# Reordering the hand-written instruction streams of a pipelined AdaLN block on one core: four engines' call orders and the banks of shared PSUM units

## The reference

```python
mod = (silu(c) @ wmod).reshape(8, 6, 1, -1)            # sa, ca, ga, sb, cb, gb
h = layernorm(x) * (1 + ca) + sa
q, k, v = rope(h @ Wq), rope(h @ Wk), h @ Wv
ck, cv = compress(k + pe), compress(v + pe)            # 16 tokens into one
imp = (q · ck).mean(heads, queries); idx = top_k(imp, 2)
out = g0 * attend(q, ck, cv) + g1 * attend(q, k[idx], v[idx]) + g2 * window_attend(q, k, v, 128)
x = x + ga * (out @ Wo + bo)                           # g = softmax(h @ Wg + bg)
h = layernorm(x) * (1 + cb) + sb
x = x + gb * (h @ W.T + b + shared(h) + top2_routed(h))
```

## Time and profile before

| what | us |
|---|---|
| median of the three runs (2274.74 to 2276.2) | 2275.06 |
| span of the profiled execution | 2265.8 |
| the profiled execution's own time beside its span: the runs' median less the span | 9.3 |
| TensorE busy in the span | 2108.9 (93%) |
| VectorE busy | 1698.7 (75%) |
| ScalarE busy | 1331.8 (59%) |
| GpSimd busy | 792.1 (35%) |

### The profile page before, as it was taken

The page is one execution under the profiler, slowest core; times in us unless marked ns, Lnnn a source line. Parts: engine busy times, 40 slices in busy tenths (PEclk is TensorE's granted clock), DMA queues, the critical chain, the costliest instruction groups (busy, mean ns, idle before and its releaser), DMA issues.

```text
span 2265.8 us, 49116 instructions
## 1 busy us (share of the span) xinstructions
PE 2108.9 (93%) x17948; PEld 1398.6 (62%) x17948; DVE 1698.7 (75%) x4741; ACT 1331.8 (59%) x4706; POOL 792.1 (35%) x780
## 2 busy tenths in 40 slices
PE   6989999999999999999999999999999999997887
PEld 3656666566665666656665666656666566664454
DVE  4667777777876887777887777777787688776775
ACT  2346666656664665656665665655666566565554
POOL 2433333433334333333343333343333333333121
PEclk9999999999999999999999999999999999998999
DMA  6110000200011000110002000020001100021000
GB/s 219 55 34 25 20 29 29 70 30 29 24 49 55 25 20 30 52 47 29 29 24 75 29 19 26 29 70 29 29 25 52 52 25 20 29 52 38 20 21 19
DMA packets 49022, 89.66 MB, mean 40 GB/s; under 512 B 6888, under 2 KB 6888, under 8 KB 48784
## 3 DMA queue, kind: packets, MB, share of 16 engines
q1 hardware_dynamic: 37520, 68.95, 9.9%
q10 hardware_dynamic: 11264, 17.57, 2.1%
HBM read 69.68 MB, written 16.83 MB: 38 GB/s over the span
## 4 chain that ended last, share of the span: by engine, by line
PE 57%; DVE 26%; ACT 7%; issue 6%; POOL 3%; DMA 1%; SPq 0%; DVEq 0%; POOLq 0%; ACTq 0%
PE ps_m L719 9%; PE ps_o L651 7%; PE ps_m L684 5%; ACT pw L1093 5%; DVE ps_s L1632 4%; PE ps_s L645 4%; PE ps_m L523 4%; PE ps_m L525 4%; PE ps_m L524 4%; PE ps_t L627 4%; DVE wmax L1637 3%; PE ps_m L701 3%; PE ps_s L603 2%; DVE cden L1692 2%; DVE pT L1660 2%
## 5 line engine op out<-in xcount | busy, mean ns | idle before, releaser
L1093 ACT ACTIVATE pw<-ps_s,wmax 128x128 f32<-128x128 f32 x1024 | 359.1, 379 | 241.1 <-DVE wmax L1637 240.1
L523 PE MATMUL ps_m<-w_hi,h_hi 128*128 128x512 f32 x768 | 368.1, 479 | 4.0 <-DVE h_lo L1763 1.4
L1103 ACT ACTIVATE pw<-pw,wden 128x128 f32<-128x128 f32 x1024 | 313.8, 401 | 6.5 <-DVE wden L1647 6.1
L525 PE MATMUL ps_m<-w_hi,h_lo 128*128 128x512 f32 x768 | 303.6, 395 | 0.0
L524 PE MATMUL ps_m<-w_lo,h_hi 128*128 128x512 f32 x768 | 303.6, 395 | 0.0
L684 PE MATMUL ps_m<-wo_s,aT 128*128 128x512 f32 x512 | 259.3, 628 | 6.4 <-ACT v_s L1058 3.7
L719 PE MATMUL ps_m<-wbt_s,h2T 128*128 128x512 f32 x512 | 252.2, 612 | 0.0
L1127 ACT ACTIVATE pT<-ps_s 80x512 f32<-80x512 f32 (+6 forms) x224 | 133.0, 594 | 182.2 <-PE ps_s L645 171.5
L1093 ACT ACTIVATION_READ_ACCUMULATOR pw<-ps_s,wmax 128x1 f32 x1024 | 224.6, 219 | 0.0
L1658 DVE COPY_PREDICATED pT<-keep_prev,ps_t 128x512 f32<-128x512 uint32 x224 | 163.8, 731 | 52.9 <-PE ps_t L627 51.5
L1345 POOL TENSOR_TENSOR css<-css,cm 128x256 f32<-128x256 f32 (+7 forms) x128 | 110.9, 887 | 258.6 <-DVE cm L1684 258.6
(11 more groups left out here) (196 smaller groups left out, 4219.5 us busy)
## 6 DMA issues: line engine op xcount, KB each, us to landing
xa<-x_in SPq DMA_DIRECT2D x65, 256.0 KB, 2.9
xc<-x_in SPq DMA_DIRECT2D x64, 256.0 KB, 2.7
out<-t ACTq DMA_DIRECT2D x64, 256.0 KB, 2.1
wo_s<-wo_in SPq DMA_DIRECT2D x8, 1024.0 KB, 9.3
wbt_s<-wbt_in SPq DMA_DIRECT2D x8, 1024.0 KB
gbc<-gate_rows SPq DMA_DIRECT2D x24, 256.0 KB, 5.2
pw<-wmod_in SPq DMA_DIRECT2D x3, 1024.0 KB, 8.0
pT<-wmod_in SPq DMA_DIRECT2D x3, 1024.0 KB, 9.2
```

The lines of the kernel that those rows point to most:

```text
L523: pe_.matmul(ps[:], h_hi[:, c, :], w_hi[:, col, c, :], start=(c == 0), stop=False)
L525: mm = pe_.matmul(ps[:], h_lo[:, c, :], w_hi[:, col, c, :], start=False, stop=(c == NC - 1))
L1093: ins = act.activation(pw[:, hw, :], ps_w[:, j, i, 1, :], ACT.Exp, bias=wmax[:, hw:hw + 1], accum_out=wden[:, 0, hw:hw + 1])
L1103: act.activation(pw[:, hw, :], pw[:, hw, :], ACT.Copy, scale=wden[:, 2, hw:hw + 1]).then_inc(wn_ok, 1)
```

## The change

The calls inside `first_slot`, `slot`, `turn`, `head`, `end_first`, `end_slot` and `last` are put in another order on TensorE, ScalarE, GpSimd and VectorE, and the tables of banks are set anew to fit. Each engine issues the same instructions as before, with the same operands, buffers and semaphore waits; SyncE's list isn't touched. The tables become shorter by one line, so every line of the code behind them stands one lower on TensorE's part; on the other engines added blank lines shift the numbers further (L1569 becomes L1600, for example).

The diff, cut to the parts spoken of below:

```diff
-SLOT_ORDER = [("Y", 1), ("Q", 0), ("K", 1), ("QT", 0), ("G", 0), ("H2T", 0),
-              ("Z", 1), ("F", 0), ("KT", 1), ("ZT", 1), ("V", 1), ("HT", 0)]
+SLOT_ORDER = [("Y", 1), ("Q", 0), ("K", 1), ("QT", 0), ("G", 0), ("H2T", 0), ("Z", 0), ("F", 0),
+              ("KT", 1), ("ZT", 1), ("HT", 0), ("V", 1)]
...
 TensorE, first_slot
                 window_scores(b, 1, 0)
-                project(seg, b, t, "Q", 0, [0, 1])
+                project(seg, b, t, "Q", 0, [0])
+                project(seg, b, t, "K", 1, [0, 1])
+                project(seg, b, t, "Q", 0, [1, 2, 3])
                 transpose_cs(b, 0, 0)
-                project(seg, b, t, "Q", 0, [2])
+                window_scores(b, 1, 1)
                 transpose_cs(b, 0, 1)
                 cs_values(b, 0, 0)
-                project(seg, b, t, "Q", 0, [3])
-                window_scores(b, 1, 1)
-                project(seg, b, t, "K", 1, [0])
                 transpose_cs(b, 0, 2)
-                project(seg, b, t, "K", 1, [1, 2, 3])
+                project(seg, b, t, "K", 1, [2, 3])
...
-                cs_values(b, 1, 2)
                 window_values(b, 1, 3)
+                feed(seg, b, t, [0, 1])
                 cs_values(b, 1, 3)
+                feed(seg, b, t, [2])
                 transpose_z(seg, b, t)
-                feed(seg, b, t, [3])
-                project(seg, b, t, "V", 2, [0])
-                feed(seg, b, t, [NC])
-                project(seg, b, t, "V", 2, [1, 2])
+                feed(seg, b, t, [3, NC])
+                project(seg, b, t, "V", 2, [0, 1, 2, 3])
                 transpose_h(seg, b, t + 1, Ta + 1)
-                project(seg, b, t, "V", 2, [3])
...
 TensorE, slot
-                project(seg, b, t, "K", 1, [0])
+                project(seg, b, t, "K", 1, [0, 1])
                 transpose_window(b, s, 0)
-                project(seg, b, t, "K", 1, [1])
                 transpose_rot(seg, b, t, Ta, "QT", ra, 1)
+                project(seg, b, t, "K", 1, [2])
                 gate_logits(seg, b, t, [0, 1, 2, 3])
-                project(seg, b, t, "K", 1, [2, 3])
+                project(seg, b, t, "K", 1, [3])
                 transpose_h2(seg, b, t)
                 window_values(b, s, 0)
                 transpose_window(b, s, 1)
                 transpose_cs(b, s, 0)
                 lora_down(seg, b, t)
-                feed(seg, b, t, [0, 1])
+                cs_values(b, s, 0)
+                transpose_cs(b, s, 1)
+                feed(seg, b, t, [0])
                 transpose_rot(seg, b, t, Ta, "KT", kr, 2)
-                feed(seg, b, t, [2, 3])
-                transpose_cs(b, s, 1)
+                feed(seg, b, t, [1, 2])
                 transpose_z(seg, b, t)
+                feed(seg, b, t, [3, NC])
                 transpose_window(b, s, 2)
-                cs_values(b, s, 0)
+                transpose_cs(b, s, 2)
                 window_values(b, s, 1)
                 cs_values(b, s, 1)
-                transpose_cs(b, s, 2)
-                feed(seg, b, t, [NC])
-                project(seg, b, t, "V", 2, [0])
+                transpose_h(seg, b, t + 1, Ta + 1)
                 transpose_cs(b, s, 3)
                 transpose_window(b, s, 3)
-                transpose_h(seg, b, t + 1, Ta + 1)
-                project(seg, b, t, "V", 2, [1, 2, 3])
+                project(seg, b, t, "V", 2, [0, 1, 2, 3])
                 window_values(b, s, 2)
                 cs_values(b, s, 2)
                 window_values(b, s, 3)
                 cs_values(b, s, 3)
...
 ScalarE, first_slot
                 cs_exps(b, 0)
+                window_exp(b, 1, 0)
                 probs_copy(b, 0, 0)
-                window_exp(b, 1, 0)
...
 ScalarE, slot
                 h_scaled(seg, b, t, "H2T", h2T, mod_c, modc_ok, b + 1)
+                probs_copy(b, s, 0)
+                copy_z(seg, b, t)
                 gate_exp(Ta)
-                copy_z(seg, b, t)
-                probs_copy(b, s, 0)
                 router_exp(b, t)
+                probs_copy(b, s, 1)
+                copy_kT(seg, b, t)
+                copy_zT(seg, b, t)
                 window_norm(b, s, 1)
-                copy_kT(seg, b, t)
-                probs_copy(b, s, 1)
-                copy_zT(seg, b, t)
                 probs_copy(b, s, 2)
+                store(seg, b, t)
                 probs_copy(b, s, 3)
-                store(seg, b, t)
...
 VectorE, first_slot
+                window_max(b, 1, 0)
                 cs_factor(b, 0)
-                window_max(b, 1, 0)
                 rope(seg, b, t, "Q")
...
 VectorE, slot
                 window_weights(b, s, 0)
+                ln_scale(x1[:], mvc, vec, xc[:, t % 2, :], lnc, lncp, NT * b + t)
                 rope(seg, b, t, "Q")
                 window_max(b, s, 1)
                 cs_factor(b, s)
-                ln_scale(x1[:], mvc, vec, xc[:, t % 2, :], lnc, lncp, NT * b + t)
                 gates_soft(seg, b, t, Ta, 0)
                 split_probs(b, s, 0)
                 rope(seg, b, t, "K")
+                split_probs(b, s, 1)
                 router(seg, b, t, 0)
                 window_weights(b, s, 1)
                 router(seg, b, t, 1)
-                split_probs(b, s, 1)
                 ln_a(seg, b, s - 1, Ta + 1, s)
+                final(seg, b, t)
                 split_probs(b, s, 2)
+                sum_q(seg, b, t, Ta)
+                split_probs(b, s, 3)
                 gates_soft(seg, b, t, Ta, 1)
-                final(seg, b, t)
-                split_probs(b, s, 3)
                 sum_keys(Ta, t)
-                sum_q(seg, b, t, Ta)
```

More of the change, by code:

```diff
@@ L747, in first_slot @@
                 transpose_window(b, 1, 0)
-                output(seg, b, t, [1, 2])
+                output(seg, b, t, [1, 2, 3])
                 transpose_window(b, 1, 1)
-                output(seg, b, t, [3])
+                transpose_rot(seg, b, t, Ta, "KT", kr, 2)
+                transpose_cs(b, 1, 0)
                 window_values(b, 1, 0)
-                transpose_cs(b, 1, 0)
-                transpose_rot(seg, b, t, Ta, "KT", kr, 2)
-                transpose_window(b, 1, 2)
                 transpose_cs(b, 1, 1)
                 cs_values(b, 1, 0)
-                window_values(b, 1, 1)
+                transpose_window(b, 1, 2)
                 transpose_cs(b, 1, 2)
                 transpose_h2(seg, b, t)
+                window_values(b, 1, 1)
                 cs_values(b, 1, 1)
@@ L899, in end_first @@
                 transpose_cs(b, 0, 0)
+                transpose_cs(b, 0, 1)
                 cs_values(b, 0, 0)
-                transpose_cs(b, 0, 1)
-                transpose_cs(b, 0, 2)
                 window_scores(b, 1, 1)
                 cs_values(b, 0, 1)
+                transpose_cs(b, 0, 2)
                 transpose_cs(b, 0, 3)
                 cs_values(b, 0, 2)
+                cs_values(b, 0, 3)
                 transpose_window(b, 1, 0)
-                cs_values(b, 0, 3)
+                cs_scores(b, 1)
+                window_values(b, 1, 0)
                 transpose_window(b, 1, 1)
-                cs_scores(b, 1)
-                output(seg, b, t, [0, 1])
+                output(seg, b, t, [0, 1, 2])
                 transpose_window(b, 1, 2)
-                output(seg, b, t, [2])
-                window_values(b, 1, 0)
                 output(seg, b, t, [3])
@@ L920, in end_first @@
                 transpose_h2(seg, b, t)
+                transpose_cs(b, 1, 2)
                 cs_values(b, 1, 1)
+                window_values(b, 1, 2)
                 transpose_window(b, 1, 3)
-                window_values(b, 1, 2)
-                transpose_cs(b, 1, 2)
                 lora_down(seg, b, t)
@@ L944, in end_slot @@
                 lora_down(seg, b, t)
-                feed(seg, b, t, [0, 1, 2])
+                feed(seg, b, t, [0, 1])
+                transpose_window(b, s, 1)
                 transpose_cs(b, s, 0)
-                transpose_window(b, s, 1)
-                feed(seg, b, t, [3])
+                window_values(b, s, 0)
+                feed(seg, b, t, [2])
                 transpose_cs(b, s, 1)
-                window_values(b, s, 0)
                 cs_values(b, s, 0)
@@ L953, in end_slot @@
                 transpose_window(b, s, 2)
+                feed(seg, b, t, [3])
                 transpose_z(seg, b, t)
                 transpose_cs(b, s, 2)
-                feed(seg, b, t, [NC])
+                cs_values(b, s, 1)
+                window_values(b, s, 2)
                 transpose_window(b, s, 3)
                 transpose_cs(b, s, 3)
-                cs_values(b, s, 1)
-                window_values(b, s, 2)
+                feed(seg, b, t, [NC])
                 cs_values(b, s, 2)
@@ L970, in last @@
                 lora_down(seg, b, t)
-                feed(seg, b, t, [0, 1, 2])
+                feed(seg, b, t, [0, 1, 2, 3])
                 transpose_z(seg, b, t)
-                feed(seg, b, t, [3, NC])
```

(30 more changed lines are left out.)

86 lines of the change are left out of this document (40 added, 46 removed).

## The result

The changed kernel took 2292.32 us (median, 2290.34 to 2295.21), the kernel before 2275.05: a ratio of 1.0075, interval [1.006, 1.0089]. A second comparison on another chip gave 1.0067 [1.0051, 1.0082]. The time came out within 0.5 us of the forecast, but not by the forecast's terms. The strips came out near their price and slot 2 went the right way; Tw2's wait and slots 6 and 7 were priced too high, the first slot's gain didn't come and the turn's cost was missing. The errors cancelled.

The account below looks back on a forecast made before the run. VectorE was taken to bound each slot's first half, TensorE the second. A round's terms, 6 x 0.25 + 6 x 0.25 + 0.65 - 0.25 - 1.0 = 2.4, gave 16.8 us in seven rounds: 2292, own range 2281 to 2302, overall 2258 to 2305.

Parts of the forecast that it names:

- The strips: Second half of a slot: one more block of narrow values products on TensorE costs 0.25 us a slot (0.1 to 0.5).
- slot 2: Slot 2's start: GpSimd's split ends earlier, and VectorE's small instruction with it, -0.25 us a round (-1.0 to 0.3).
- Tw2's wait: Second half of a slot: Tw2 waits for ScalarE's later window_norm, about 0.25 us in each slot (0 to 0.55).
- slots 6 and 7: Tcs0 waits for GpSimd's later product, 0.45 us in slot 7, half in slot 6: 0.65 a round (0 to 1.2).
- the first slot's gain: First slot: shorter waits at the first Tcs and second window scores, less strip blocks: -1.0 us a round (-1.9 to 0).
- the turn's cost: Turn: 0 us, within -0.45 and 0.5, from longer runs and moved products.
- First half, 0: First half of a slot: VectorE sets its end, so the first values product starts where it did, 0 us.
- NC half of its 1.02: Step in timing Tw2 in slot 4: NC counted as 0.51 us, so Tw2 could start at 8.23.
- Rival two: Slots: VectorE isn't the first half's bound and the logits' wait is won, 0.69 us a slot: 2252 us, chance 0.18.
- the dearer one: Second half: Tw3 waits too, for VectorE's split, some 0.4 us a slot, 16.8 more: 2309 us, chance 0.08.
- The first rival: Tw2 never waits (10.5 us less) and the first slot gains 1.9, not 1.0: 2275 us, no change, chance 0.18.

Follow-up runs that it names:

- a3: Changed kernel with VectorE's scaled norm back behind the cs factor in the six slots: 2303.45 us, 1.0114.
- b5: Kernel before with cv0 moved out of the block with wv1 and cv1, alone between F1 and K's transposes, in the six slots: 2288.45 us, 1.0051.
- a1: Changed kernel with cv0 moved back into the block with wv1 and cv1 in the six slots: 2289.73 us, 1.0058 of the kernel before.
- p1: Kernel before with the new order of the six slots alone, on all engines: 2287.94 us, 1.0056.
- p3: Kernel before with the new order of the first slot alone, on all engines: 2276.95 us, 1.0001.
- b7: b6 plus the changed kernel's K, QT and gate logits order in the slots, scaled norm ahead of Q's rotary embedding in slots 2 to 5: 2279.93 us, 1.0025.
- p4: Kernel before with the new order of the prologue heads and the epilogue's functions alone: 2277.48 us, 1.0005.
- b6: p3 with, in the first slot, K's transposes behind cv0 of tile 1 and the cs factor ahead of the first split: 2275.22 us, 0.9999.
- p2: Kernel before with the new order of the turn alone, on all engines: 2278.97 us, 1.0011.

## Why the prediction was right, and where not

- **First half, 0: nearly.** VectorE is the bound, and the first values product waits for its split in all 42 slots. Slots 3 to 5 still gained 0.14, 0.15 and 0.06; a3 takes them away, so the scaled norm's place brings them. The step that missed them is that VectorE had no gap but the reciprocals': it waited some 0.1 for Q there, and the norm fills that.
- **Strips, 0.25 a slot: right in size.** Second halves grew 0.27 to 0.35 in slots 2 to 6. In slot 4's rows Z, cv0 and Tcs1 hold 1.81 (1365.84 to 1367.65) where they held 0.93 + 0.24 + 0.44 = 1.61, so 0.20 of 0.29 stand at the new block, and b5 shows the block alone. Putting cv0 back gave only 0.09 (a1), so what the order costs isn't strips alone.
- **Tw2's wait, 0.25 a slot: wrong.** The step that failed is "NC half of its 1.02". The row before was followed by a chunk of V, whose start at 1363.88 and length of 0.80 hid NC's second half; F's 0.87 for two matmuls was the right model. 10.5 us of the sum didn't exist. The prediction's lower bound, 0, allowed for this.
- **Slots 6 and 7, 0.65: too large.** GpSimd's product did start 0.46 later in slot 7, counted from the slot's start, but took 2.48 us and not 2.71, so Tcs0 lost some 0.24, and slot 6 nothing.
- **Slot 2, -0.25: the right mechanism, -0.44.** VectorE's small instruction still ends with GpSimd's split (1561.23 and 1561.19), which now starts 0.61 ahead of it and not 0.17, and so takes 0.70 instead of 1.13. p1, which keeps the old first slot, has no such gain, and p3 has it: it hangs on the first slot's end, as forecast.
- **First slot, -1.0: wrong.** The two waits did as forecast: the first Tcs waits 1.00 (0.94 was worked out) and the second scores none. The step that failed is the end of the sum there: nothing was asked to be late next. The 1.3 us went to new waits, in the changed kernel 0.37, 0.60 and 0.49 (K's transposes, whose bank Y's residual still reads), and, by the reading of the rows, to strips. By p3 the slot and slot 2's gain together cost 0.2 us: nothing that can be told from no change.
- **Turn, 0: too low by 2.5 us**, inside its bounds (3.5). TensorE is busy 0.55 more in the new turn (34.52 against 33.97); edges as in the slots weren't counted there, but that they make it up is not tested. That it isn't the 0.7 a round of the two traces is told below.

Rival two (the logits' wait won) falls with the 42 waits at the values and with the first halves, which are as long as before or at most 0.15 shorter (slot 2 apart). So does the dearer one: no Tw3 of a slot is in the list of waits. The first rival had Tw2's wait rightly at nothing, but its price for the first slot was as wrong. In seven rounds, terms of +10.5 (Tw2) and +2.9 (slots 6 and 7) too many stood against 7 us of first slot that didn't come, 2.5 of turn, perhaps 1.1 at the ends, and low clock: in the trace, two rounds have 199.38 and 197.70 for the six slots, and the other five 196.6 to 196.7. That the sum met the time to a thousandth is luck; its rows say which part to believe.

The sum's base had a flaw as well. In every later run the time is 2.1 to 2.4 us above the span, not 9.3, so the first profiled execution took some 2268, 7 us less than the median that stood for it: the rows of before are those of a fast execution.

## What to carry to other kernels

Where the tail of an engine's list is its bound, count the blocks of narrow strips in it: here one more block cost 0.27 us, eleven in 42 slots, with no wait to be seen. Take a row's holding time only from a place where the same kind of row follows it as in the new order, and when a wait is taken away, ask at once which buffer or engine is late next. A wait off the bound isn't free for certain: behind one of 0.75 us, which itself cost nothing, the clock was low in seven rounds of seven (b7), though that the wait brings it on isn't shown. Before a difference of two profiles is believed, look at a second profile of the kernel before.

## What wasn't expected of the hardware

The kernel before has two lengths of turn: 34.3 to 34.7 us in all seven rounds of the first profile, 35.4 in four of seven in the second. In six other traces with this turn (p1, p3, p4, b5, b6, b7) 2, 0, 6, 7, 3 and 5 of the seven are long. What differs is which of two instructions is held up, VectorE's scaled norm or GpSimd's weighing of the keys. A long turn, VectorE and GpSimd:

```profile
1219.05 1.65 DVE L1569 TENSOR_SCALAR xc<-x,mvc,vec 128x512 f32<-128x512 f32 x1
...
1219.14 1.27 POOL L1385 TENSOR_TENSOR ra<-kT,wrow 128x512 f32<-128x512 f32 x1
```

A short one of the same execution:

```profile
1488.66 0.55 DVE L1569 TENSOR_SCALAR xc<-x,mvc,vec 128x512 f32<-128x512 f32 x1
...
1488.77 1.58 POOL L1385 TENSOR_TENSOR ra<-kT,wrow 128x512 f32<-128x512 f32 x1
```

The starts are 0.1 apart in both, and one of the two instructions pays: 1.1 us on VectorE, which H2T then waits 1.0 for, or 0.3 on GpSimd, for which TensorE doesn't wait. In the 27 long turns of the eight traces it is VectorE each time, in the 29 short ones GpSimd.

In the long one VectorE's row starts 0.09 ahead and still loses, so the Trainium skill's rule that whichever issues first has the pair of ports (SBUF — State Buffer, section Who interferes with whom) fits the exclusion, but a row's start doesn't tell who issued first. In the new turn GpSimd's row starts 0.4 ahead and VectorE's takes 1.18 each time, with no wait of H2T behind it; the turn is 35.1 always. With half of the old turns long, their mean is some 34.9 (an estimate from the eight traces), so the new one costs about 0.2 a round, 1.4 us: within p2's 0.5 to 4.6, and well under 7 x 0.7. Single runs of the kernel before, 2270 to 2279 us, hold such tosses.
